# Transposing one token tile a second time in plain f32 and comparing the two results, in the expert phase of a two-layer decoder kernel

## The chip, the cores and the metric

The kernel runs on one core of one Trainium2 chip. The metric is the device time of one execution in microseconds (us). The time before is the median of three runs. A profile of one further execution, taken by the hardware profiler, gives the rows shown below; its times count from the first instruction of the execution.

## The reference

Six sublayers act on x of 16 x 128 tokens with 512 features; each adds its result to x and normalizes the row. The last one, the only one that the change touches, is a mixture of experts:

```
logits = x @ gate_weight.T
topk_w, topk_idx = top_k(softmax(logits), 2)
combine = zeros(T, 8).at[arange(T)[:, None], topk_idx].add(topk_w)
gu  = einsum('th,efh->tef', x, gate_up_weights)
act = silu(gu[..., :352]) * gu[..., 352:]
y   = einsum('tef,te,ehf->th', act, combine, down_weights)
sgu = x @ shared_gate_up.T
y   = y + (silu(sgu[:, :704]) * sgu[:, 704:]) @ shared_down.T
x   = layernorm(x + y)
```

## The kernel before

Each sublayer is a phase, written by hand for the five engines; an instruction waits on semaphores (`wait_ge`) and counts them up (`then_inc`). The shared part of the last sublayer is a phase of its own, which also routes the tokens: it writes each token's row twice to a DRAM buffer `x_slots`, sorted by expert, so that 39 tiles of 128 rows arise (`TILES`), each of which belongs to one expert.

`expert_ffn_phase` then works through these 39 tiles. Matrix products are made in three parts, from a rounded high half and a low half of each operand (`products`, lines 97 to 99; high halves end in `h`, low ones in `l`). For a tile i the steps are:

- SP loads the rows into `xin[:, i % 4, :]` (tile 0 is already in `first_x`).
- PE transposes them in four 128 x 128 blocks into the PSUM bank `tr` (`transposes`, L2147; tile 0 at L2149), and counts `tr_full` up at the last block.
- ACT copies `tr` to `xgh` (the rounded high half, L2048, counting `tr_hi`); DVE subtracts that from `tr` and writes the low half `xgl` (`tokens`, L2085, counting `tr_lo`).
- PE multiplies by the gate and the up weights (`ups`, 12 products of 352 columns each), ACT applies silu (L2063), DVE multiplies by the up part to `hf` (L2093).
- PE transposes `hf` into the bank `ht` (L2194), ACT and DVE split it to `hth` (L2071) and `htl` (L2099).
- PE multiplies by the down weights into `yb[i % 2]` (`down`, 9 products of 512 columns), ACT scales it to `ys` (L2055), SP stores it in `y_slots`.

The order on PE is fixed by the loop at the end of the function, and is a tile deep in software pipelining: `ups` of tile i, the transposes of tile i + 1, `down` of tile i - 1, the transposes of `hf` of tile i. On DVE it is `hf` of tile i, `tokens(i + 1)`, `htl` of tile i. In the first turn of the loop there is no `down`:

```
transposes(0)
...
pe.wait_ge(tr_lo, i + 1)
...
ups(gate[i % 2], i, ring, 0).then_inc(gate_full, 1)
...
    transposes(i + 1)
if i >= 1:
    down(i - 1, rings[i - 1][0])
```

POOL splits the weights of the coming experts meanwhile (L2006, L2009). After the tiles POOL fetches each token's two results from `y_slots`: the first set is added to `X` by indirect DMAs (L2033, counting `low_added`), the second goes to `yg`, which lies in the weights' buffers (L2036, counting `yg_in`). DVE adds `yg` (L2117), computes the statistics (L2120, L2123), ACT normalizes (L2076), SP stores the 16 blocks.

Of the kernel before, what the change touches and what calls it, by code (L numbers as in the profile page):

```python
# [7 lines left out]
ALU = mybir.AluOpType  # L8
ACT = mybir.ActivationFunctionType
AX = mybir.AxisListType.X  # L10

P = 128
B = 16
DM = 512
C = DM // P
# [79 lines left out]
def products(pe, out, wh, wl, xh, xl, first, last, **kw):  # L95

    pe.matmul(out, wh, xh, start=first, stop=False, **kw)  # L97
    pe.matmul(out, wh, xl, start=False, stop=False, **kw)  # L98
    return pe.matmul(out, wl, xh, start=False, stop=last, **kw)  # L99
# [57 lines left out]
class Phase:  # L157
# [8 lines left out]
    def sb(self, name, shape, dt=F32):  # L166
        return self.ctx.enter_context(self.nc.sbuf_tensor(f"{self.name}_{name}", shape, dt))

    def sem(self, name):
        self.sems.append(self.ctx.enter_context(self.nc.semaphore(f"{self.name}_{name}")))  # L170
        return self.sems[-1]
# [31 lines left out]
def four(bank):  # L203

    return bank[:, :].rearrange("p (c n) -> p c n", n=P)


def f32(ap):
    return ap.bitcast(F32)
# [1703 lines left out]
def expert_ffn_phase(nc, S, w):  # L1913
# [6 lines left out]
    NX = 4  # L1920
    sets = [(0, 4), (4, 8), (8, 12), (12, 14), (14, 16)]
    with Phase(nc, "expert") as phase:
        sb, sem = phase.sb, phase.sem
# [3 lines left out]
        xin, identr = sb("xin", [P, NX, DM], F32R), sb("identr", [P, P], F32R)  # L1927
# [9 lines left out]
        gate, up, yb, tr, ht = S.bank[0:2], S.bank[2:4], S.bank[4:6], S.bank[6], S.bank[7]  # L1937
# [7 lines left out]
        yg_in = [sem(f"yg_in{b}") for b in range(B)]  # L1945
        high_added = sem("high_added")
        w_hi, w_ready, tile_done, spare_set = sem("w_hi"), sem("w_ready"), sem("tile_done"), sem("spare_set")
        ident_rounded = sem("ident_rounded")
        tr_full, tr_hi, tr_lo = sem("tr_full"), sem("tr_hi"), sem("tr_lo")
        gate_full, up_full, sig_done, hf_done = sem("gate_full"), sem("up_full"), sem("sig_done"), sem("hf_done")  # L1950
        ht_full, ht_hi, ht_lo = sem("ht_full"), sem("ht_hi"), sem("ht_lo")
# [127 lines left out]
        @block.vector  # L2079
        def _(dve):  # L2080
            def tokens(i):
                dve.wait_ge(tr_hi, i + 1)
                if i >= 2:
                    dve.wait_ge(up_full, i - 1)
                dve.tensor_tensor(xgl[:, i % 2, :, :], four(tr), f32(xgh[:, i % 2, :, :]), ALU.subtract).then_inc(tr_lo, 1)  # L2085

            tokens(0)
            for i in range(TILES):
                dve.wait_ge(sig_done, i + 1)
                dve.wait_ge(up_full, i + 1)  # L2090
                if i >= 2:
                    dve.wait_ge(ht_full, i - 1)
                dve.tensor_tensor(hf[:, i % 2, :], sg[:, i % 2, :], up[i % 2][:, 0:F1], ALU.mult).then_inc(hf_done, 1)  # L2093
                if i + 1 < TILES:
                    tokens(i + 1)
                dve.wait_ge(ht_hi, i + 1)
                if i >= 2:
                    dve.wait_ge(tile_done, i)
                dve.tensor_tensor(htl[:, i % 2, :], ht[:, 0:HW], f32(hth[:, i % 2, :]), ALU.subtract).then_inc(ht_lo, 1)  # L2099

            def spread(k):
                lo, hi = sets[k]
                dve.wait_ge(mv_done, hi)
                dve.tensor_scalar(ve[:, lo:hi], mv[:, lo:hi, 1], EPS, None, ALU.add).then_inc(ve_done, 1)

            def shifts(k):
                lo, hi = sets[k]
                dve.wait_ge(rs_done, k + 1)
                dve.scalar_tensor_tensor(out=shift[:, lo:hi], in0=mv[:, lo:hi, 0], scalar=-1.0, in1=rs[:, lo:hi],
                                         op0=ALU.mult, op1=ALU.mult).then_inc(shift_done, 1)  # L2110

            ends = [hi - 1 for lo, hi in sets]
            for n in range(B + 2):
                if n < B:
                    dve.wait_ge(low_added[n], 16)
                    dve.wait_ge(yg_in[n], 16)
                    dve.tensor_tensor(S.X[:, n, :], S.X[:, n, :], yg[n], ALU.add).then_inc(high_added, 1)  # L2117
                if 1 <= n <= B:
                    dve.wait_ge(high_added, n)
                    dve.bn_stats(out=six[:, n - 1, :], in_=S.X[:, n - 1, :]).then_inc(six_done, 1)  # L2120
                if n >= 2:
                    dve.wait_ge(six_done, n - 1)
                    dve.bn_aggr(out=mv[:, n - 2, :], in_=six[:, n - 2, :]).then_inc(mv_done, 1)  # L2123
                    if n - 2 in ends:
                        spread(ends.index(n - 2))
                if n - 4 in ends:
                    shifts(ends.index(n - 4))
            for k in range(len(sets)):
                if ends[k] + 4 >= B + 2:
                    shifts(k)  # L2130

        @block.tensor
        def _(pe):
            def owner(i):
                ring = pe.value_load(S.ring[0:1, i:i + 1], min_val=0, max_val=2)
                order = pe.value_load(S.owner1[0:1, i:i + 1], min_val=1, max_val=E)
                return ring, order

            def transposes(i):
                if i:  # L2140
                    pe.wait_ge(ident_rounded, 1)
                    pe.wait_ge(x_in[i % NX], 16 * (i // NX + (i % NX > 0)))
                    pe.wait_ge(tr_lo, i)
                for c in range(C):
                    cols = slice(c * P, (c + 1) * P)
                    if i:
                        m = pe.transpose(tr[:, cols].bitcast(F32R), xin[:, i % NX, cols], identr[:, :])  # L2147
                    else:
                        m = pe.transpose(tr[:, cols], S.first_x[:, cols], S.ident[:, :])  # L2149
                m.then_inc(tr_full, 1)  # L2150

            def moving(t, ring, lo, n, r=P):
                return t[0:r, bass.ds(ring, 1), lo:lo + n].rearrange("p a n -> p (a n)")

            def ups(dst, i, ring, col):
                for c in range(C):
                    at = c * 2 * F1 + col
                    m = products(pe, dst[:, 0:F1], xgh[:, i % 2, c, :], xgl[:, i % 2, c, :],
                                 moving(weh, ring, at, F1), moving(wel, ring, at, F1), c == 0, c == C - 1)
                return m  # L2160

            def down(i, ring):
                pe.wait_ge(ht_lo, i + 1)
                if i >= 2:
                    pe.wait_ge(y_copied, i - 1)
                for j in range(J):
                    r, cols = FT[j], slice(j * P, (j + 1) * P)
                    m = products(pe, yb[i % 2], hth[0:r, i % 2, cols], htl[0:r, i % 2, cols],
                                 moving(weh, ring, WU + j * DM, DM, r), moving(wel, ring, WU + j * DM, DM, r),
                                 j == 0, j == J - 1)  # L2170
                m.then_inc(tile_done, 1)

            transposes(0)
            rings = [owner(0)]
            for i in range(TILES):
                ring, order = rings[i]
                pe.wait_ge(w_ready, order)
                pe.wait_ge(tr_lo, i + 1)
                if i >= 2:
                    pe.wait_ge(sig_done, i - 1)  # L2180
                ups(gate[i % 2], i, ring, 0).then_inc(gate_full, 1)
                if i >= 2:
                    pe.wait_ge(hf_done, i - 1)
                ups(up[i % 2], i, ring, F1).then_inc(up_full, 1)
                if i + 1 < TILES:
                    rings.append(owner(i + 1))
# [3 lines that stand above are left out]
                pe.wait_ge(hf_done, i + 1)  # L2190
                if i >= 1:
                    pe.wait_ge(ht_lo, i)
                for j in range(J):
                    m = pe.transpose(ht[0:FT[j], j * P:(j + 1) * P], hf[:, i % 2, j * P:j * P + FT[j]], S.ident[:, :])  # L2194
                m.then_inc(ht_full, 1)
            down(TILES - 1, rings[TILES - 1][0])
# [202 lines left out]
```

## Time and profile before

| | us |
|---|---|
| median of three runs (2100.69, 2104.23, 2106.11) | 2104.23 |
| the profiled execution, its own time | 2101.43 |
| its span, first to last instruction | 2099.6 |
| PE busy | 1930.7 (92%) |
| DVE busy | 1043.2 (50%) |
| ACT busy | 713.4 (34%) |
| POOL busy | 388.3 (18%) |
| mean granted TensorE clock, share of full | 0.970 |

The expert phase begins with PE's first transpose at 1789.4 us of the span; the last product of the last tile ends at 2055.0, the span at 2099.6. "Busy" is the time in which an engine has an instruction in work. PE stands for matrix products and transposes, PEld for its weight loads, which overlap PE. The granted clock tells how much of TensorE's full clock (2.4 GHz) the chip let through; it has two levels, 1.0 (2.4 GHz) and 0.5 (1.2 GHz), and a value between them is a stretch that holds both.

### The profile page before, as it was taken

The numbers are of one execution on the slowest core, as the hardware profiler recorded it, in microseconds if no ns is written. First come the engines' busy times: TensorE is split into PE (matmuls) and PEld (weight loads), VectorE is DVE, ScalarE is ACT, GpSimd is POOL, SyncE is SP. The second block draws the span as 40 slices with busy tenths as digits, with TensorE's granted clock in tenths as the row PEclk, the third lists the DMA queues.
The fourth block names the chain that finished last, engine by engine and source line by source line (L and its number), as shares of the span: only waits on it lengthen the run. The fifth ranks groups of instructions, "written<-read, shape, count | busy, mean of one in ns | idle before, by whom it ended". The sixth has DMA issues, their size and how long they took to land. (4 is left out here: it accounts for less than half of the span.)

```text
span 2099.6 us, 32791 instructions
## 1 busy us (share of the span) xinstructions
PE 1930.7 (92%) x12124; PEld 1574.2 (75%) x12124; DVE 1043.2 (50%) x1836; ACT 713.4 (34%) x2276; POOL 388.3 (18%) x339
## 2 busy tenths in 40 slices
PE   8999888999999979999899999999979997899991
PEld 6777576788888757877678887777758875799990
DVE  5676753455555455333455456667756232222224
ACT  4555624344444332212221111445542121233332
POOL 2110100000000046000021100000104332644335
PEclk9999999999999999999999999899999998899996
DMA  7211051000000021000290001000014200644257
GB/s 237 59 42 41 3 190 51 1 1 1 1 1 1 1 106 61 0 0 0 88 393 6 1 31 41 1 2 1 2 46 158 93 0 0 226 140 164 79 115 206
DMA packets 73375, 135.89 MB, mean 65 GB/s; under 512 B 13456, under 2 KB 31760, under 8 KB 71184
## 3 DMA queue, kind: packets, MB, share of 16 engines
q1 hardware_dynamic: 47376, 96.28, 13.3%
q0 software_dynamic: 7888, 27.94, 4.5%
q10 hardware_dynamic: 17968, 9.71, 1.8%
q8 instruction: 96, 1.57, 0.3%
q14 instruction: 47, 0.39, 0.1%
HBM read 90.62 MB, written 43.29 MB: 64 GB/s over the span
## 5 line engine op out<-in xcount | busy, mean ns | idle before, releaser
L1470 PE MATMUL banks<-ternary_xth,ternary_wq 128*128 (+1 forms) x352 | 139.3, 396 | 5.7 <-DVE ternary_wq L1401 3.6
L1470 PE MATMUL banks<-ternary_xtl,ternary_wq 128*128 (+1 forms) x352 | 138.1, 392 | 0.0
L571 ACT ACTIVATE causal_pr<-banks,causal_nb 128x128 f32<-128x128 f32 x256 | 90.1, 379 | 53.0 <-DVE causal_nb L713 53.0
L97 PE MATMUL banks<-latent_vh,latent_cth 128*128 128x512 f32 x256 | 104.3, 407 | 3.5 <-DVE latent_ctl L1171 3.5
L97 PE MATMUL banks<-weights,expert_xgh 128*128 x312 | 104.4, 334 | 2.3 <-DVE expert_xgl L2085 2.3
L571 ACT ACTIVATE gqa_pr<-banks,gqa_nb 128x128 f32<-128x128 f32 x256 | 90.1, 383 | 45.4 <-DVE gqa_nb L713 45.4
L99 PE MATMUL banks<-weights,expert_xgl 128*128 x312 | 101.2, 324 | 0.0
L98 PE MATMUL banks<-weights,expert_xgh 128*128 x312 | 101.1, 324 | 0.0
L98 PE MATMUL banks<-latent_vl,latent_cth 128*128 128x512 f32 x256 | 100.3, 392 | 0.0
L99 PE MATMUL banks<-latent_vh,latent_ctl 128*128 128x512 f32 x256 | 100.1, 391 | 0.0
L1124 ACT ACTIVATE latent_pt<-banks 128x1024 f32<-128x1024 f32 x32 | 32.9, 1027 | 187.8 <-PE banks L1270 187.8
L1430 DVE TENSOR_TENSOR ternary_hf<-ternary_sg,banks 128x512 f32<-128x512 f32 x44 | 30.2, 686 | 133.7 <-issue 80.1
L1371 ACT ACTIVATE ternary_sg<-banks 128x512 f32<-128x512 f32 x44 | 26.3, 598 | 190.2 <-PE banks L1470 190.2
L1085 POOL TENSOR_TENSOR latent_rs<-latent_ve,mhalf 128x1 f32<-128x1 f32 x15 | 8.3, 551 | 444.5 <-DVE latent_ve L219 444.5
L1115 ACT ACTIVATE latent_pr<-banks,latent_nb 128x128 f32<-128x128 f32 x256 | 90.2, 373 | 0.0
L97 PE MATMUL banks<-latent_xgh,latent_ch 128*128 128x256 f32 x256 | 77.2, 302 | 9.4 <-DVE latent_xgl L1165 4.6
L1470 PEld LDWEIGHTS banks<-ternary_xth,ternary_wq 128*128 128x128 f32 x352 | 66.4, 189 | 23.6 <-DVE ternary_xtl L70 4.9
L1171 DVE TENSOR_TENSOR latent_ctl<-banks,latent_cth 128x512 fp32r<-128x512 f32 x64 | 42.8, 689 | 71.6 <-ACT latent_cth L1102 71.6
L1482 PE MATMUL banks<-ternary_wq,ternary_hh 128*128 128x512 f32 x176 | 70.6, 401 | 8.1 <-DVE ternary_hl L1434 5.8
L1470 PEld LDWEIGHTS banks<-ternary_xtl,ternary_wq 128*128 128x128 f32 x352 | 66.4, 189 | 13.9
L743 DVE TENSOR_TENSOR X<-X,banks 128x512 f32<-128x512 f32 x48 | 33.0, 687 | 81.3 <-PE banks L99 81.3
L98 PE MATMUL banks<-latent_xgl,latent_ch 128*128 128x256 f32 x256 | 72.3, 283 | 0.0
(463 smaller groups left out, 5487.4 us busy)
## 6 DMA issues: line engine op xcount, KB each, us to landing
x_slots<-decay_zeros SPq DMA_DIRECT2D x39, 256.0 KB, 4.0
y_slots<-decay_zeros SPq DMA_DIRECT2D x39, 256.0 KB, 4.2
y_slots<-expert_ys SPq DMA_DIRECT2D x39, 256.0 KB
expert_xin<-x_slots SPq DMA_DIRECT2D x38, 256.0 KB, 2.9
weights_raw<-in_expert_experts SPq DMA_DIRECT2D x4, 2176.0 KB, 9.1
gqa_tw<-in_ternary_w ACTq DMA_DIRECT2D x4, 2112.0 KB
ternary_raw<-in_ternary_w SPq DMA_DIRECT2D x11, 768.0 KB, 4.1
expert_raw<-in_expert_experts POOLq DMA_DIRECT2D x3, 2176.0 KB, 10.0
```

What stands on the lines that cost most here:

```text
L97: pe.matmul(out, wh, xh, start=first, stop=False, **kw)
L98: pe.matmul(out, wh, xl, start=False, stop=False, **kw)
L99: return pe.matmul(out, wl, xh, start=False, stop=last, **kw)
L571: a = act.activation(pr[:, h, c, :], S.bank[2 * h + c // 4][:, (c % 4) * P:(c % 4 + 1) * P], ACT.Exp, bias=nb[:, h, c:c + 1], accum_out=su ...
L743: dve.tensor_tensor(row, row, bank, ALU.add).then_inc(free_d, 1)
L1115: a = act.activation(pr[:, c, :], S.bank[x][:, j * P:(j + 1) * P], ACT.Exp, bias=nb[:, c:c + 1], accum_out=sums[:, c:c + 1])
L1124: act.activation(pt[:, :, :], pair(1), ACT.Copy).then_inc(pt_done, 1)
L1171: dve.tensor_tensor(ctl[:, x, :], S.bank[2 + x], f32(cth[:, x, :]), ALU.subtract).then_inc(ct_lo, 1)
L1371: act.activation(sg[:, j % 2, :], gate[j % 2][:, :], ACT.Sigmoid).then_inc(sig_done, 1)
L1430: dve.tensor_tensor(hf[:, j % 2, :], sg[:, j % 2, :], up[j % 2][:, :], ALU.mult).then_inc(hf_done, 1)
L1470: a = pe.matmul(dst[:, :], wq[:, j, m, c * P:(c + 1) * P], x[:, c, toks], start=c == 0 and n == 0, stop=c == C - 1 and n == 1)
L1482: a = pe.matmul(yb[i][:, :], h[:, j % 2, i * P:(i + 1) * P], wq[:, j, 2, :], start=j == 0 and n == 0, stop=j == J - 1 and n == 1)
```

## The change

Tile 1 is treated differently from the other 38. After its four transposes on the rounded f32r type, PE makes the same four on plain f32, into the bank `yb[1]` (PSUM bank 5), and only the last of these counts `tr_full`. DVE then runs five instructions ahead of the `xgl` of tile 1: it copies `tr` to SBUF, subtracts `yb[1]`, squares, takes the maximum over each row of 512, and writes 1e4 or 0 to `wrong`, per partition. Each of the first four counts `off_chain`, and the next waits for it. Much later, ahead of the add of `yg[0]`, DVE adds `wrong` to column 0 of block 0 of `X` and waits for that. The buffers `off`, `most` and `wrong` and the semaphores `off_done` and `off_chain` are new; the buffers are declared behind all others of the phase.

```diff
@@ -1945,7 +1945,8 @@
         yg_in = [sem(f"yg_in{b}") for b in range(B)]
         high_added = sem("high_added")
         w_hi, w_ready, tile_done, spare_set = sem("w_hi"), sem("w_ready"), sem("tile_done"), sem("spare_set")
-        ident_rounded = sem("ident_rounded")
+        ident_rounded, off_done, off_chain = sem("ident_rounded"), sem("off_done"), sem("off_chain")
+        off, most, wrong = sb("off", [P, DM]), sb("most", [P, 1]), sb("wrong", [P, 1])
         tr_full, tr_hi, tr_lo = sem("tr_full"), sem("tr_hi"), sem("tr_lo")
         gate_full, up_full, sig_done, hf_done = sem("gate_full"), sem("up_full"), sem("sig_done"), sem("hf_done")
         ht_full, ht_hi, ht_lo = sem("ht_full"), sem("ht_hi"), sem("ht_lo")
@@ -2082,6 +2083,16 @@
                 dve.wait_ge(tr_hi, i + 1)
                 if i >= 2:
                     dve.wait_ge(up_full, i - 1)
+                if i == 1:
+                    dve.tensor_copy(off[:, :], tr).then_inc(off_chain, 1)
+                    dve.wait_ge(off_chain, 1)
+                    dve.tensor_tensor(off[:, :], off[:, :], yb[1], ALU.subtract).then_inc(off_chain, 1)
+                    dve.wait_ge(off_chain, 2)
+                    dve.tensor_tensor(off[:, :], off[:, :], off[:, :], ALU.mult).then_inc(off_chain, 1)
+                    dve.wait_ge(off_chain, 3)
+                    dve.tensor_reduce(most[:, :], off[:, :], AX, ALU.max).then_inc(off_chain, 1)
+                    dve.wait_ge(off_chain, 4)
+                    dve.tensor_scalar(wrong[:, :], most[:, :], 0.0, 1e4, ALU.is_gt, ALU.mult).then_inc(off_done, 1)
                 dve.tensor_tensor(xgl[:, i % 2, :, :], four(tr), f32(xgh[:, i % 2, :, :]), ALU.subtract).then_inc(tr_lo, 1)
 
             tokens(0)
@@ -2113,6 +2124,10 @@
             for n in range(B + 2):
                 if n < B:
                     dve.wait_ge(low_added[n], 16)
+                    if n == 0:
+                        dve.wait_ge(off_done, 1)
+                        dve.tensor_scalar(S.X[:, 0, 0:1], S.X[:, 0, 0:1], wrong[:, 0:1], None, ALU.add).then_inc(off_done, 1)
+                        dve.wait_ge(off_done, 2)
                     dve.wait_ge(yg_in[n], 16)
                     dve.tensor_tensor(S.X[:, n, :], S.X[:, n, :], yg[n], ALU.add).then_inc(high_added, 1)
                 if 1 <= n <= B:
@@ -2147,6 +2162,10 @@
                         m = pe.transpose(tr[:, cols].bitcast(F32R), xin[:, i % NX, cols], identr[:, :])
                     else:
                         m = pe.transpose(tr[:, cols], S.first_x[:, cols], S.ident[:, :])
+                if i == 1:
+                    for c in range(C):
+                        cols = slice(c * P, (c + 1) * P)
+                        m = pe.transpose(yb[1][:, cols], f32(xin[:, i % NX, cols]), S.ident[:, :])
                 m.then_inc(tr_full, 1)
 
             def moving(t, ring, lo, n, r=P):
```

On PE, from the load of tile 1's owner on, the order before:

```order
L2135 ISA x2
L2136 TENSOR_LOAD owner
L2136 ISA x2
L2147 MATMUL banks<-expert_identr,expert_xin 128x128 x4
L2194 MATMUL banks<-ident,expert_hf 128x128 x2
L2194 MATMUL banks<-ident,expert_hf 96x128
L97 ISA
L97 MATMUL banks<-weights,expert_xgh 128x352
```

and in the changed kernel:

```order
L2150 ISA x2
L2151 TENSOR_LOAD owner
L2151 ISA x2
L2162 MATMUL banks<-expert_identr,expert_xin 128x128 x4
L2168 MATMUL banks<-ident,expert_xin 128x128 x4
L2213 MATMUL banks<-ident,expert_hf 128x128 x2
L2213 MATMUL banks<-ident,expert_hf 96x128
L97 ISA
L97 MATMUL banks<-weights,expert_xgh 128x352
```

The four plain transposes stand between those of tile 1 and those of tile 0's `hf`; the first product behind them is the gate product of tile 1.

On DVE, from the phase's first instruction on, the order before:

```order
L2085 TENSOR_TENSOR expert_xgl<-banks,expert_xgh 128x512
L2093 TENSOR_TENSOR expert_hf<-expert_sg,banks 128x352
L2085 TENSOR_TENSOR expert_xgl<-banks,expert_xgh 128x512
L2099 TENSOR_TENSOR expert_htl<-banks,expert_hth 128x384
L2093 TENSOR_TENSOR expert_hf<-expert_sg,banks 128x352
```

and in the changed kernel:

```order
L2096 TENSOR_TENSOR expert_xgl<-banks,expert_xgh 128x512
L2104 TENSOR_TENSOR expert_hf<-expert_sg,banks 128x352
L2087 COPY expert_off<-banks 128x512
L2089 TENSOR_TENSOR expert_off<-expert_off,banks 128x512
L2091 TENSOR_TENSOR expert_off<-expert_off 128x512
L2093 TENSOR_REDUCE expert_most<-expert_off 128x1
L2095 TENSOR_SCALAR expert_wrong<-expert_most 128x1
L2096 TENSOR_TENSOR expert_xgl<-banks,expert_xgh 128x512
L2110 TENSOR_TENSOR expert_htl<-banks,expert_hth 128x384
L2104 TENSOR_TENSOR expert_hf<-expert_sg,banks 128x352
```

The five new instructions stand ahead of tile 1's `xgl`; `htl` of tile 0 and `hf` of tile 1 are queued behind it.

## Rows read from the trace of the kernel before

**Rows 1.** The page, the chain that ended last, its shares by engine.

```profile
PE 12%; POOL 1%; DMA 0%; DVE 0%; ACT 0%; issue 0%; ACTq 0%; DVEq 0%
```

**Rows 2.** Windows of the expert phase: busy us, then PEclk, DMA share, GB/s.

```profile
core 0: us, PE busy (x) PEld busy (x) DVE busy (x) ACT busy (x) POOL busy (x), PEclk, DMA share, GB/s
1799.80:2051.00 251.20, 251.17 (x1516) 233.37 (x1516) 66.43 (x113) 79.60 (x150) 122.35 (x67) 1.00 0.47 142
```

**Rows 3.** Waits of PE from 1787 us on: us in total, times, longest.

```profile
PE banks L97 <- DVE expert_xgl L2085: 2.3, 2, 1.6
```

**Rows 4.** Timeline around tile 1's transposes: start us, us, engine, operation.

```profile
1797.75 0.46 PE L2147 MATMUL banks<-expert_identr,expert_xin 128*128 128x128 f32 x4
1798.03 0.52 DVE L2093 TENSOR_TENSOR expert_hf<-expert_sg,banks 128x352 f32<-128x352 f32 x1 [6.16 <-PE banks L99]
1798.25 0.60 ACT L2048 ACTIVATE expert_xgh<-banks 128x512 fp32r<-128x512 f32 x1 [1.82 <-PE banks L2147]
...
1798.61 0.55 PE L2194 MATMUL banks<-ident,expert_hf 128*128 128x128 f32 x3 [0.39 <-DVE expert_hf L2093]
1798.88 0.69 DVE L2085 TENSOR_TENSOR expert_xgl<-banks,expert_xgh 128x512 fp32r<-128x512 f32 x1 [0.33 <-ACT expert_xgh L2048]
...
1799.83 0.42 PE L97 MATMUL banks<-weights,expert_xgh 128*128 x1 [0.67 <-DVE expert_xgl L2085]
```

**Rows 5.** Windows in a run of plain f32 transposes (L60).

```profile
1553.00:1556.00 3.00, 3.00 (x16) 3.00 (x15) 1.89 (x3) 2.08 (x4) 0.00 (x0) 0.50 0.94 257
...
1557.00:1560.00 3.00, 3.00 (x30) 3.00 (x29) 2.84 (x6) 2.99 (x7) 0.00 (x0) 1.00 0.91 389
```

**Rows 6.** Groups of DVE by line and form: xcount, busy us, mean ns.

```profile
L713 DVE TENSOR_REDUCE gqa_nb<-banks 128x8 f32<-128x1024 f32 x32 | 39.2, 1224 | 16.9 <-PE banks L864 16.1
...
L1175 DVE COPY latent_qt<-banks 128x512 f32<-128x512 f32 x32 | 22.1, 691 | 70.4 <-PE banks L99 70.4
...
L1804 DVE TENSOR_TENSOR shared_hf<-shared_sg,banks 128x512 f32<-128x512 f32 x20 | 13.7, 686 | 68.7 <-PE banks L99 58.9 <-issue 9.8
...
L2117 DVE TENSOR_TENSOR X<-X,weights_raw 128x512 f32<-128x512 f32 x8 | 5.5, 689 | 12.1 <-DMA weights_raw<-y_slots,pos 11.9
...
L219 DVE TENSOR_SCALAR causal_ve<-causal_mv 128x1 f32<-128x1 f32 x16 | 2.5, 154 | 0.5
...
L1695 DVE TENSOR_REDUCE shared_mx<-first_x 128x16 f32<-128x128 f32 x1 | 0.3, 285 | 0.0
```

**Rows 7.** Timeline of DVE: L1140 waits for L1139 by a semaphore.

```profile
307.89 0.42 DVE L1139 TENSOR_TENSOR latent_pt<-ahead_kv,latent_kvr 128x256 f32<-128x256 f32 x1
308.34 0.42 DVE L1140 TENSOR_TENSOR ahead_kv<-latent_pt 128x256 f32<-128x256 f32 x1
```

**Rows 8.** Timeline of DVE: L2120 does not wait for the L2117 ahead.

```profile
2082.40 0.69 DVE L2117 TENSOR_TENSOR X<-X,expert_raw 128x512 f32<-128x512 f32 x1 [0.64 <-DMA expert_raw<-y_slots,pos]
2083.01 0.69 DVE L2120 BATCH_NORM_STATS2 expert_six<-X 128x6 f32<-128x512 f32 x1
```

**Rows 9.** Windows: gaps of PE, and stretches at a half clock behind them.

```profile
250.00:252.00 2.00, 0.00 (x0) 0.00 (x0) 0.89 (x2) 2.00 (x14) 0.00 (x0) 1.00 0.02 4
252.00:257.00 5.00, 4.84 (x18) 3.77 (x19) 2.45 (x4) 0.63 (x3) 0.78 (x1) 0.66 0.02 3
...
398.50:401.00 2.50, 0.00 (x0) 0.00 (x0) 1.39 (x3) 1.74 (x9) 0.11 (x1) 1.00 0.00 0
401.00:403.00 2.00, 1.89 (x16) 1.92 (x17) 0.00 (x0) 0.00 (x0) 0.00 (x0) 1.00 0.00 0
...
1304.50:1314.00 9.50, 9.50 (x49) 7.82 (x50) 5.31 (x7) 5.57 (x28) 0.21 (x1) 0.50 0.61 210
...
1547.00:1552.00 5.00, 0.00 (x0) 0.00 (x0) 2.30 (x7) 0.00 (x0) 0.55 (x1) 0.79 0.00 0
1552.00:1557.00 5.00, 4.97 (x25) 5.00 (x26) 2.90 (x5) 2.83 (x5) 0.00 (x0) 0.52 0.77 243
```

**Rows 10.** Timeline of DVE: its first add after the tiles.

```profile
2063.64 0.69 DVE L2117 TENSOR_TENSOR X<-X,weights_raw 128x512 f32<-128x512 f32 x1 [11.14 <-DMA weights_raw<-y_slots,pos]
```

## The prediction

> **What bounds the kernel now.** I read the chain that ended last first. Its engine shares begin in the expert phase, and of them PE has 12% of the span, POOL 1%, everything else about nothing [rows 1]: there, PE sets the end. The windows say the same more sharply. From the gate product of tile 1 to the last tiles PE is busy for 251.17 of 251.20 us, at a clock of 1.00, while DVE is busy for 66.43 and ACT for 79.60 [rows 2]. So from that product on there is no slack on PE in which a delay could be made good: what is late at 1799.83 is late at the end. DVE, in contrast, is idle for three quarters of the time, and the same five instructions in most other places of the phase would cost nothing. Everything hangs on the place.
>
> The place is the first turn of the software pipeline, before there is a `down` to fill PE's time. PE's only waits for an `xgl` in this phase are the two of tiles 0 and 1, 2.3 us in total, 1.6 the longer [rows 3], hence 0.7 for tile 1. The timeline shows how this comes about [rows 4]: PE's transposes of tile 1 end at 1798.21, ACT's high half runs from 1798.25 to 1798.85, DVE's `xgl` from 1798.88 to 1799.57, and 0.26 later PE starts the gate product at 1799.83. PE itself was done with the transposes of tile 0's `hf` at 1799.16. It is therefore the chain of transposes, ACT, DVE that PE waits for, and the change puts work into two links of it. From tile 2 on, `down` of an earlier tile stands between the transposes and the gate product and covers that chain; those tiles are left as they are.
>
> **The change, part by part.**
>
> *Four plain f32 transposes on PE.* A run of such transposes passes 30 in 3.00 us at the full clock and 16 in 3.00 at the half [rows 5], 0.10 and 0.19 us each. The four f32r transposes ahead take 0.46 us together [rows 4], less than four at the half clock could, so the clock is full and `tr_full` comes 4 x 0.10 = 0.40 us later; bounds are 0.4 and, at a half clock, 0.75. PE's own time is not lengthened by them: `hf` is ready only at 1798.55 [rows 4], and the four start their work at about 1798.1 and have been passed by then.
>
> *Five instructions on DVE, each behind the one before.* The copy of 512 elements from PSUM takes 0.691, the subtraction with one operand in PSUM 0.686, the product of two SBUF operands 0.689 (as the add of L2117). The row maximum has no row of its size; between 128 elements in SBUF at 0.285 and 1024 in PSUM at 1.224 it comes by a straight line to 0.69. The comparison on 128 x 1 takes 0.154 [rows 6]. What the four waits add is seen where L1140 waits for L1139: 0.42 of work, the next start after 0.45, so 0.03 each [rows 7]. Without a wait, the next 512-element instruction starts after 0.61 of the 0.69 [rows 8]. So four steps of 0.69 + 0.03 make 2.88 us, and the fifth, for which `xgl` does not wait, 0.154 - 0.08 = 0.07: together 2.95 us.
>
> Here a page can be set against the rows. The Trainium skill, "VectorE: DVE Perf Modes", section "The DRAIN you can't avoid", says of chained Vector instructions that the semaphore after each of them costs nothing extra, as the pipeline empties after each anyhow. By that the step would be the 0.61 of the unwaited pair and the five would come to about 2.5 us, 0.44 less. The rows of this kernel speak against it, since waited and unwaited pairs differ by 0.11 us.
>
> *Queue behind them.* On DVE `htl` of tile 0 and `hf` of tile 1 stand behind the five. `htl` would end at about 1803.5; `down(0)`, which needs it, comes after 24 more products and the next transposes, which PE starts only after `xgl`. `hf` of tile 1 needs the up product, later still. On ACT nothing new stands ahead of `hth`. SP's load of tile 4 waits for `tr_full` of tile 0, and POOL's weight split for a DMA; neither is touched. All these I cost at nothing, with 3 to 4 us of products as their cover.
>
> *The late add on DVE.* It waits for `off_done`, long since set, and for `low_added[0]`. DVE then stands idle for 11.14 us until its first add at 2063.64, because `yg[0]` has yet to land [rows 10]. A 128 x 1 instruction of 0.154 lies inside that; without the cover it would cost 0.2. Two more semaphores to clear at the end are instructions with no visible time. Nothing depends on what the comparison finds: the instruction list has no branch, so a differing word would change the output and no time.
>
> *Sum of the delay:* 0.40 + 2.95 = 3.35 us. PE's gap ahead of the gate product of tile 1 grows from 0.67 to 4.0 us.
>
> *The clock.* That gap is long by this kernel's measure. A gap of 2.0 us at 250 was followed by a stretch in which the granted clock averages 0.66 over 5 us, which is 2 x 0.34 x 5 = 3.4 us at the half level. A gap of 5.0 us at 1547 saw the clock fall within it (mean 0.79, so 2.1 us at the half level, the fall 2.9 us after its start) and then 4.8 us of half clock (0.52 over 5 us). But a gap of 2.5 us at 398.5 left it at 1.00 [rows 9]. With 4.0 us, beyond 2.9, I expect the fall. What it costs is the share of the work that is not done: 16 transposes instead of 30 in the same time is a loss of 0.47. Bounds: 0 (the gap of 2.5) and 4.8 x 0.47 = 2.3 us; I take the 3.4 us of the first case, 1.6 us, since the restart here meets the same unbroken work as there.
>
> The Trainium skill, "TensorE: Matmul & The Clock Gate", section "Terms", puts the penalty at throttled time times one minus the clock ratio, one half. By that the 3.4 us would cost 1.7, and the sum would be 0.1 more; the rows give 0.47, as the part of the time that does not follow the clock would have it.
>
> Total: 3.35 + 1.6 = 5.0 us. The profiled execution's own time of 2101.43 would become 2106.4. It lies 2.8 below the median of the three runs, to which I apply the same sum: 2104.23 + 5.0 = **2109.2 us**, 0.24% more. About 0.3% (6.3 us) is what a measurement of this kernel can tell from no change; the three runs alone differ by 5.4.
>
> **The rivals.**
>
> *The clock does not fall.* The gap of 2.5 us that passed without effect speaks for it, the 5.0 that did not against. Then only the delay counts: +3.35, 2107.6.
>
> *The half clock lasts long, and the change is measurably slower.* Place: tiles 1 and 2, right behind the gap. From 1304.5 to 1314.0 PE was busy throughout and the clock stayed at 0.50 [rows 9]. The same here costs 9.5 x 0.47 = 4.5 us on top: +7.8, 2112.0. It decides once the half clock lasts longer than (6.3 - 3.35) / 0.47 = 6.3 us. For it: it happened in this trace. Against: behind the other two gaps it lasted 3.4 and 4.8 us, and the work here is an unbroken row of full products.
>
> *The delay is absorbed.* That would be so if something other than PE set the end, say POOL's first set of gathers or the landing of the last stores. Against it speaks the absence of slack on PE [rows 2], and that these gathers wait for the same tiles. +0, 2104.2.
>
> *The memory or code layout shifts something elsewhere.* The buffers come last and the phases ahead have the same instructions; this could go either way, by no more than the scatter of the runs: 2102 to 2106.
>
> **How the numbers follow.** My forecast, one fall of the clock that lasts 2 to 5 us, gets 0.68; no fall 0.14; the long half clock 0.09; absorbed 0.06; layout 0.03. The predicted time is that of the first. Range: at the low end the delay with the shorter steps of 0.61 (2.9 us), no clock term, less 2 us for the scatter of a median of such runs: 2105. At the high end 3.35 + 2.3, plus those 2: 2111.9, which takes in the long half clock at 2112. So 2105 to 2112. Slower by over 0.3%: the long half clock whole, 0.09, a quarter of the forecast, where a high clock term and scatter meet, 0.16, and 0.01 of layout, 0.26. Faster by over 0.3%: 0.02, from scatter and layout. The same: 0.72.
>
> **What would show it.** In the changed kernel's timeline: ACT's high half of tile 1 0.4 us later against the transposes before it; five new DVE instructions in some 3 us; PE's wait for `xgl` of tile 1 near 4.0 instead of 0.7; the next window after it at a clock of 0.50 for some 3 us, with products at nearly double spacing; then tiles at the old pace to the end; and the first add after the tiles still behind the landing of `yg[0]`. I am wrong if PE's gap is under 2 us, if tiles after the second run slower than before, or if the end does not move with the last tile.

## The result, and the profile after

The changed kernel took 2112.21 us in the median of 18 runs (2105.34 to 2116.25), the kernel before 2104.87 in 18 runs beside them (2100.69 to 2110.09). The ratio is 1.0029, with a 95% interval from 1.0019 to 1.0040, which is +6.1 us (4.0 to 8.4) on 2105. The forecast was 2109.2, from 2105 to 2112, and "the same within 0.3%" at 0.72. So direction and order are right, and the size is at the upper side: the delay and the clock together, forecast at 5.0 us, lie inside the interval, but below its middle. The ratio is taken from all runs; the two medians alone differ by 7.3 us. The median of 2112.21 itself is 0.2 us above the stated range. The ratio of +0.29% is just inside "the same within 0.3%", and its interval reaches beyond that.

On the page of the changed kernel, busy time of the engines and the shares of the chain that ended last read as before [rows 1]: PE still sets the end.

```profile
PE 1935.6 (92%) x12128; PEld 1578.6 (75%) x12128; DVE 1047.6 (50%) x1842; ACT 711.7 (34%) x2276; POOL 388.1 (18%) x339
...
PE 12%; POOL 1%; DVE 1%; DMA 0%; ACT 0%; issue 0%; ACTq 0%; DVEq 0%
```

The profiled execution has a span of 2112.7 us, 13.1 more than the one before. Most of that isn't the change's, which is why I cut both spans at three instructions: T0, the start of tile 0's transposes; the start of tile 1's gate product, A behind T0; the start of the last tile's down products, B behind that; and the end, C behind that. D is the last part of A, from the first f32r transpose of tile 1 on.

| | T0 | A | of which D | B | C |
|---|---|---|---|---|---|
| before | 1789.43 | 10.40 | 2.08 | 252.81 | 46.96 |
| changed | 1796.32 | 14.12 | 5.50 | 254.25 | 48.01 |
| difference | 6.89 | 3.72 | 3.42 | 1.44 | 1.05 |

A and B are where the change acts, 5.16 us together. The timeline of PE, ACT and DVE around tile 1 answers to [rows 4]; square brackets hold the time for which the engine was idle just before the instruction, and what ended it:

```profile
1804.94 0.46 PE L2162 MATMUL banks<-expert_identr,expert_xin 128*128 128x128 f32 x4
1805.24 0.63 PE L2168 MATMUL banks<-ident,expert_xin 128*128 128x128 f32 x4
1805.80 0.55 PE L2213 MATMUL banks<-ident,expert_hf 128*128 128x128 f32 x3
1805.90 0.60 ACT L2049 ACTIVATE expert_xgh<-banks 128x512 fp32r<-128x512 f32 x1 [2.50 <-PE banks L2168]
...
1806.53 0.69 DVE L2087 COPY expert_off<-banks 128x512 f32<-128x512 f32 x1 [0.79 <-ACT expert_xgh L2049]
1807.26 0.69 DVE L2089 TENSOR_TENSOR expert_off<-expert_off,banks 128x512 f32<-128x512 f32 x1
1807.98 0.69 DVE L2091 TENSOR_TENSOR expert_off<-expert_off 128x512 f32<-128x512 f32 x1
1808.70 0.69 DVE L2093 TENSOR_REDUCE expert_most<-expert_off 128x1 f32<-128x512 f32 x1
1809.43 0.15 DVE L2095 TENSOR_SCALAR expert_wrong<-expert_most 128x1 f32<-128x1 f32 x1
1809.50 0.68 DVE L2096 TENSOR_TENSOR expert_xgl<-banks,expert_xgh 128x512 fp32r<-128x512 f32 x1
1810.10 0.55 DVE L2110 TENSOR_TENSOR expert_htl<-banks,expert_hth 128x384 fp32r<-128x384 f32 x1
...
1810.44 0.66 PE L97 MATMUL banks<-weights,expert_xgh 128*128 x1 [4.09 <-DVE expert_xgl L2096]
```

From the first f32r transpose to ACT's start it is 0.96 us, where it was 0.50: the four plain ones cost 0.46. From ACT's start to the start of `xgl` it is 3.60, where it was 0.63: the five instructions cost 2.97. Each 512-element one starts 0.72 after the one before and lasts 0.69, and `xgl` starts 0.07 after the comparison. Together with 0.01 less from `xgl` to PE that is D's 3.42. The remaining 0.30 of A comes before all that: the clock rose later within tile 0's products, and tile 1's transposes began 8.62 behind T0 instead of 8.32. PE's wait grew from 0.7 to 4.1 (in total, with tile 0's, from 2.3 [rows 3] to 5.7), and behind it the clock is at its half level for 0.32 x 2 x 5 = 3.2 us of the next 5:

```profile
PE banks L97 <- DVE expert_xgl L2096: 5.7, 2, 4.1
```

```profile
core 0: us, PE busy (x) PEld busy (x) DVE busy (x) ACT busy (x) POOL busy (x), PEclk, DMA share, GB/s
1806.44:1810.44 4.00, 0.00 (x1) 0.01 (x1) 3.77 (x7) 0.44 (x2) 2.17 (x2) 0.97 1.01 435
1810.44:1815.44 5.00, 5.00 (x22) 5.00 (x23) 0.20 (x1) 0.46 (x1) 5.00 (x3) 0.68 0.37 150
1815.44:2062.00 246.56, 246.45 (x1491) 229.12 (x1490) 65.98 (x112) 78.61 (x148) 114.41 (x63) 1.00 0.44 134
```

In the first of these windows PE is idle, and the clock falls some 0.2 us before its end. In the second PE passes 22 matmuls in 5 us, where the kernel before passed 32 in the 5 us behind its own gap. In the third the clock is at 1.00 and PE has practically no gaps, as in [rows 2]. B is longer by 1.44, and this stretch is the only one in it that differs.

The late add lies where it was expected, right behind DVE's last `htl` and ahead of the idle time before the first add. It took 0.20 us and nothing waited for it:

```profile
2063.99 0.56 DVE L2110 TENSOR_TENSOR expert_htl<-banks,expert_hth 128x384 fp32r<-128x384 f32 x1 [2.60 <-ACT expert_hth L2072]
2064.46 0.20 DVE L2129 TENSOR_SCALAR X<-X,expert_wrong 128x1 f32<-128x1 f32 x1
2075.86 0.69 DVE L2132 TENSOR_TENSOR X<-X,weights_raw 128x512 f32<-128x512 f32 x1 [11.19 <-DMA weights_raw<-y_slots,pos]
```

The two other differences, T0 and C, are looked at below.

### The profile page after: what moved, and what is told of

Same layout as the page of the kernel before. It is cut to its first block and busy times, and to the rows that moved or that the text cites. A ratio compares the mean times of both kernels' runs of the same rounds, so it can differ in the third digit from the quotient of the medians.

```text
span 2112.7 us, 32808 instructions
## 1 busy us (share of the span) xinstructions
PE 1935.6 (92%) x12128; PEld 1578.6 (75%) x12128; DVE 1047.6 (50%) x1842; ACT 711.7 (34%) x2276; POOL 388.1 (18%) x339
```

## The experiments

Eleven runs were made, two of them repeats (e4 of the changed kernel, e5 of the one before), each with a profile, in which the cuts were made as above. They ran on three chips: e1 to e4 on one where the kernel before takes 2104.39 us, e5 to e8 on one where it takes 2112.95, e9 to e11 on one where it takes 2105.04. Each ratio is against the runs of the kernel before on the same chip. The edits are shown against the changed kernel.

| | T0 | A | D | PE's gap | B | C | ratio (95%) |
|---|---|---|---|---|---|---|---|
| e1 declarations only | 1790.37 | 10.68 | 2.06 | 0.67 | 252.81 | 48.34 | 1.0005 (0.9993 to 1.0017) |
| e2 check behind xgl | 1793.71 | 10.37 | 2.08 | 0.67 | 252.53 | 48.09 | 1.0005 (0.9994 to 1.0016) |
| e3 gap filled | 1795.96 | 14.01 | 5.38 | 0.26 | 253.12 | 48.31 | 1.0018 (1.0005 to 1.0031) |
| e4 changed, again | 1796.99 | 15.74 | 6.34 | 4.94 | 254.00 | 48.87 | 1.0026 (1.0012 to 1.0039) |
| e5 before, again | 1798.14 | 11.01 | 2.07 | 0.67 | 252.78 | 48.17 | 1.0001 (0.9988 to 1.0014) |
| e6 nine instructions | 1797.67 | 22.59 | 13.80 | 12.40 | 255.31 | 48.63 | 1.0070 (1.0044 to 1.0095) |
| e7 nine, from PSUM | 1800.64 | 16.57 | 8.37 | 6.97 | 253.98 | 48.61 | 1.0030 (1.0016 to 1.0044) |
| e8 copy alone ahead | 1797.89 | 11.32 | 3.13 | 1.73 | 252.80 | 48.19 | 1.0010 (0.9994 to 1.0027) |
| e9 PE part only | 1792.77 | 11.35 | 2.54 | 1.13 | 252.67 | 48.41 | 1.0006 (0.9993 to 1.0019) |
| e10 DVE part only | 1792.70 | 14.16 | 5.02 | 3.62 | 255.11 | 47.53 | 1.0040 (1.0023 to 1.0057) |
| e11 not-equal | 1786.31 | 14.06 | 4.77 | 3.36 | 254.18 | 47.95 | 1.0019 (1.0005 to 1.0033) |

**Is anything else of the change in the time?** First the declarations without the instructions:

```diff
-                if i == 1:
-                    dve.tensor_copy(off[:, :], tr).then_inc(off_chain, 1)
...
-                    if n == 0:
-                        dve.wait_ge(off_done, 1)
...
-                if i == 1:
-                    for c in range(C):
...
```

> Only the three buffers and two semaphores of the change are declared; no instruction of it is issued (the comparison and the late add are left out). Theory (delay of 3.7 us on PE's path ahead of tile 1's gate product, plus the clock): no difference, 0 us, A (start of tile 0's transposes to start of tile 1's gate product) 10.4 us as before, within 0.3 for where the clock rises. Rival (layout, two more semaphores to clear, moved code): the part of the measured +6.1 us that the delay and the clock do not explain, 1 to 3 us, shows here.

Measured: ratio 1.0005, A 10.68, B 252.81. No layout term of 1 to 3 us is seen, though the interval (-1.5 to +3.6 us) alone wouldn't exclude a small one. The kernel before once more, for a second profile:

> The kernel before once more, for a second profile of it. Both theories: A 10.4 to 10.7 us, B 252.8. Theory (run scatter outside the stretch that the change touches): tile 0's transposes start anywhere from 1789 to 1797 us, and the stretch C from the last tile's down products to the end is 47 to 49 us, as in the changed kernels. Rival (the change lengthens C by 1 us or more): C is 47.0 again.

T0 is 1798.14 here (on the second chip) and C 48.17, later and longer than in the changed kernel. C was 47.53 to 48.87 in all profiles but the first, with or without the change (48.34 in e1, 48.17 here); the 46.96 of the first was the exception, and the change adds nothing there. T0 depends on the execution: on the third chip e11, with four of the five DVE instructions, has 1786.31, earlier than the kernel before in its first profile, while e9 and e10 have 1792.77 and 1792.70; on the second, e6 and e8 have 1797.67 and 1797.89, about as the unchanged e5. The profiled executions of the changed kernel (2114.52), e3 (2113.49) and e4 (2117.41) were also among the longer ones of their kernels, and the first one of the kernel before (2101.43) among the shorter. The strongest evidence is e2 below, which issues every instruction of the change and whose ratio leaves at most 3.4 us. So the 6.9 us ahead of the expert phase aren't the change's either. A moved too in the unchanged kernel, to 11.01, by when the clock rises within tile 0's products; D is 2.07 and stands still. The part that the change makes in the first pair of profiles is thus 3.42 in D and 1.44 in B, 4.9 us.

**The same work elsewhere.** The plain transposes count their own semaphore, and the comparison stands behind `xgl`:

```diff
...
+                dve.tensor_tensor(xgl[:, i % 2, :, :], four(tr), f32(xgh[:, i % 2, :, :]), ALU.subtract).then_inc(tr_lo, 1)
                 if i == 1:
+                    dve.wait_ge(off_full, 1)
                     dve.tensor_copy(off[:, :], tr).then_inc(off_chain, 1)
...
-                dve.tensor_tensor(xgl[:, i % 2, :, :], four(tr), f32(xgh[:, i % 2, :, :]), ALU.subtract).then_inc(tr_lo, 1)
...
+                if i == 2:
+                    pe.wait_ge(off_chain, 1)
...
+                m.then_inc(tr_full, 1)
                 if i == 1:
                     for c in range(C):
                         cols = slice(c * P, (c + 1) * P)
                         m = pe.transpose(yb[1][:, cols], f32(xin[:, i % NX, cols]), S.ident[:, :])
-                m.then_inc(tr_full, 1)
+                    m.then_inc(off_full, 1)
```

> The whole comparison is kept, but the plain transposes count a semaphore of their own, so that tr_full comes when it did, and the five DVE instructions stand behind tile 1's xgl; PE's transposes of tile 2 wait for the copy. Theory: A goes back to 10.4 us, PE's wait for xgl of tile 1 to 0.7, no fall of the clock, the run within 1 us of the kernel before. Rival (the instructions cost by themselves, wherever they stand): +3 us or more stays.

Measured: A 10.37, B 252.53, ratio 1.0005 (-1.3 to +3.4 us). All instructions of the change run, and neither A nor B is longer. PE starts the gate product as early after `xgl` as before, while DVE goes on with the copy:

```profile
1803.13 0.69 DVE L2086 TENSOR_TENSOR expert_xgl<-banks,expert_xgh 128x512 fp32r<-128x512 f32 x1 [0.33 <-ACT expert_xgh L2049]
1803.74 0.68 DVE L2089 COPY expert_off<-banks 128x512 f32<-128x512 f32 x1
1804.45 0.69 DVE L2091 TENSOR_TENSOR expert_off<-expert_off,banks 128x512 f32<-128x512 f32 x1
```

```profile
1804.08 0.42 PE L97 MATMUL banks<-weights,expert_xgh 128*128 x1 [0.67 <-DVE expert_xgl L2086]
```

The place costs, not the work, as far as A and B tell.

**The clock by itself.** PE gets something to do in the gap:

```diff
                 pe.wait_ge(w_ready, order)
+                if i == 1:
+                    for _ in range(34):
+                        pe.transpose(yb[0][:, 0:P], S.ident[:, :], S.ident[:, :])
                 pe.wait_ge(tr_lo, i + 1)
```

> The changed kernel with 34 transposes of the identity into the free bank yb[0] on PE, issued ahead of the wait for tile 1's xgl, about 3.4 us of work inside the gap of 4.1. Theory (two terms): A stays at 14.1, the clock stays at 1.00 behind it, and B (start of tile 1's gate product to start of the last tile's down products) is 252.8 us as before instead of 254.3; the run comes out at +3.7 against before. Rival (the clock fall is no consequence of the gap): B stays at 254.3 and the run at +5 to +6.

```profile
1805.97:1809.97 4.00, 3.74 (x36) 3.51 (x34) 3.66 (x7) 0.55 (x2) 1.52 (x2) 1.00 1.01 426
1809.97:1814.97 5.00, 5.00 (x31) 4.85 (x32) 0.84 (x2) 1.04 (x2) 5.00 (x3) 1.00 0.42 174
```

D is 5.38, so the delay stays, but the clock stays at 1.00 and PE passes 31 matmuls in the 5 us behind the gap instead of 22. B is 253.12, 1.1 below the changed kernel's. The ratio of 1.0018 is +3.8 us (1.1 to 6.5). So the clock's fall is a consequence of the gap, and its price in the profiles is 1.1 to 1.4 us. A shorter gap is the other test:

```diff
                     dve.tensor_copy(off[:, :], tr).then_inc(off_chain, 1)
+                dve.tensor_tensor(xgl[:, i % 2, :, :], four(tr), f32(xgh[:, i % 2, :, :]), ALU.subtract).then_inc(tr_lo, 1)
+                if i == 1:
                     dve.wait_ge(off_chain, 1)
...
-                dve.tensor_tensor(xgl[:, i % 2, :, :], four(tr), f32(xgh[:, i % 2, :, :]), ALU.subtract).then_inc(tr_lo, 1)
```

> Only the copy stays ahead of tile 1's xgl, the other four instructions stand behind it; the plain transposes are still counted in tr_full. Theory (delay adds up, the clock falls only in a long gap): 0.46 for the transposes and 0.61 for the copy, A 11.4 to 11.8 us, PE's gap 1.7 us, the clock stays at 1.00, B 252.8, +1.1 us against before. Rival (a gap of 1.7 us is enough for a fall): B 254 and +2.6.

A gap of 1.73 us left the clock alone, and B is 252.80. D is 3.13, 1.05 more than before; 0.46 + 0.61 were expected. That A is only 0.3 above the 11.01 of e5 comes from the clock, which rose earlier here. The ratio of 1.0010 doesn't tell +1.1 from nothing. Gaps of 1.1 and 1.7 us (e9, e8) left the clock at 1.00, and gaps of 3.4 us and more were followed by a fall. Between them lie only [rows 9], which go both ways: behind 2.0 us it fell, behind 2.5 it didn't.

**The two halves of the delay.** PE's part alone, with the comparison and the late add left out:

```diff
-                if i == 1:
-                    dve.tensor_copy(off[:, :], tr).then_inc(off_chain, 1)
...
-                    if n == 0:
-                        dve.wait_ge(off_done, 1)
...
```

> Only the four plain transposes are added, with tr_full at their last; the five DVE instructions and the late add are left out. Theory: ACT's high half of tile 1 starts 0.96 us after the first f32r transpose instead of 0.50, PE's gap is 1.1 instead of 0.7, A 10.8 to 11.5 with where the clock rises, no fall of the clock, B 252.8, +0.5 us in all. Rival (plain f32 transposes cost four times the columns, 0.2 us each): 1.3 us instead of 0.50.

DVE's part alone, with the plain transposes left out and the subtraction taking `tr`:

```diff
-                    dve.tensor_tensor(off[:, :], off[:, :], yb[1], ALU.subtract).then_inc(off_chain, 1)
+                    dve.tensor_tensor(off[:, :], off[:, :], tr, ALU.subtract).then_inc(off_chain, 1)
...
-                if i == 1:
-                    for c in range(C):
-                        cols = slice(c * P, (c + 1) * P)
-                        m = pe.transpose(yb[1][:, cols], f32(xin[:, i % NX, cols]), S.ident[:, :])
```

> Only the five DVE instructions and the late add; the plain transposes are left out and the subtraction takes tr in place of yb[1]. Theory: from the start of ACT's high half of tile 1 to the start of xgl 3.60 us instead of 0.63, PE's gap 3.6 us, the clock falls in or behind it, A 13.3 to 14 (plus 0.4 to 1.2 if the product meets POOL's first instruction), B 253.8 to 255, +4 to +5 us. Rival (3.6 us is short enough to leave the clock alone): B 252.8 and +3.

With PE's part, ACT started at 1802.54, 0.96 behind the first transpose at 1801.58: 0.46 more than before, and not the rival's 1.3. PE's gap was 1.13; D is 2.54, 0.46 more. With DVE's part, `xgl` started at 1805.93, 3.60 behind ACT's start at 1802.33; D is 5.02, 2.94 more. Both terms are alone what they are together. B of 255.11 holds the clock and 0.7 us of a different kind: ACT's last `ys` but one waited 4.2 us for a store to land, and PE's last wait for `htl` was 2.2 instead of 1.5. Its ratio of 1.0040 is +8.4 us (4.8 to 12.0), from six runs, where 4 to 5 was expected. D and B explain 5.2 of it (2.9 and 2.3); the rest stays open. The ratio lies above the whole change's 1.0029, but the two intervals overlap.

**A product that took 1.54 us.** The changed kernel once more was meant as a repetition:

> The changed kernel once more, beside the others on one chip. Theory: A 13.8 to 14.1, the clock falls in or behind the gap and the half level lasts 2 to 5 us behind it, B 253.8 to 255.1, +5 us against before (4.5 to 6). Rival (something outside the expert phase takes 1 to 3 us more): the start of tile 0's transposes or the stretch behind the last tile is later than in the kernel before, again, by the same amount as in the first profile (6.9 and 1.1 us).

B is 254.00 as expected, but A is 15.74 and the gap 4.94. Part of it is the clock: tile 1's transposes begin 9.40 behind T0. The other part is in D, 6.34 instead of 5.50: of DVE's five, the third took more than twice its time, just when POOL had begun to split the next expert's weights:

```profile
1808.70 0.69 DVE L2089 TENSOR_TENSOR expert_off<-expert_off,banks 128x512 f32<-128x512 f32 x1
1809.42 1.54 DVE L2091 TENSOR_TENSOR expert_off<-expert_off 128x512 f32<-128x512 f32 x1
1811.00 0.69 DVE L2093 TENSOR_REDUCE expert_most<-expert_off 128x1 f32<-128x512 f32 x1
```

```profile
1809.03 4.53 POOL L2007 CAST weights<-expert_raw 128x1450 fp32r<-128x1450 f32 x3 [11.91 <-DMA expert_raw<-in_expert_experts]
```

This product is the one instruction of the five with two full operands in SBUF. In the first profile it had begun at 1807.98, 0.29 ahead of POOL's start at 1808.27, and took 0.69. There it was POOL that paid, and in e10, where the product was 0.12 ahead, as well: the first cast took 1.65 and 1.82 us instead of 1.39.

```profile
L2007 POOL CAST weights<-expert_raw 128x1450 fp32r<-128x1450 f32 x1 | 1.7, 1653 | 11.8 <-DMA expert_raw<-in_expert_experts 11.8
```

```profile
L2007 POOL CAST weights<-expert_raw 128x1450 fp32r<-128x1450 f32 x1 | 1.8, 1824 | 11.7 <-DMA expert_raw<-in_expert_experts 11.7
```

In e3 the product was done before POOL began, and no cast took over 1.40. I took the product for an instruction that POOL can hold up, and made the meeting certain in one kernel and impossible in the other: four more products of `off` with itself, and the same with the second operand of all five in PSUM.

```diff
                     dve.wait_ge(off_chain, 4)
+                    dve.tensor_tensor(off[:, :], off[:, :], off[:, :], ALU.mult).then_inc(off_chain, 1)
+                    dve.wait_ge(off_chain, 5)
...
                     dve.tensor_scalar(wrong[:, :], most[:, :], 0.0, 1e4, ALU.is_gt, ALU.mult).then_inc(off_done, 1)
```

> Four more products of off with itself (both operands in SBUF) in the chain ahead of tile 1's xgl, nine instructions in place of five. Theory A (a DVE instruction with two SBUF operands that meets POOL's weight split is held until POOL's instruction is done, which took 1.54 us in place of 0.69 in the run before): several of the five products take 1.2 to 2 us, A is 19 to 22 us, well over 14.1 + 2.9 = 17.0. Theory B (the 1.54 was a chance event): each stays at 0.69 and A is 17.0. Either way the clock falls within the gap and B is 253.8 to 255.2.

> As the run before it, but the second operand of all five products is the PSUM bank yb[1]. Theory A (only a second SBUF operand meets POOL): each product takes 0.69, A is 17.0 us, however POOL works beside it. Theory B (any DVE work beside POOL is slowed): as in the run before, over 19. The clock falls within the gap of 7 us, B 254 to 255.2.

Groups of DVE and POOL by line, with both operands in SBUF:

```profile
L2101 DVE TENSOR_TENSOR expert_off<-expert_off 128x512 f32<-128x512 f32 x1 | 3.6, 3611 | 0.0
L2007 POOL CAST weights<-expert_raw 128x1450 fp32r<-128x1450 f32 x1 | 1.8, 1774 | 11.9 <-DMA expert_raw<-in_expert_experts 11.9
L2097 DVE TENSOR_TENSOR expert_off<-expert_off 128x512 f32<-128x512 f32 x1 | 1.8, 1764 | 0.0
L2099 DVE TENSOR_TENSOR expert_off<-expert_off 128x512 f32<-128x512 f32 x1 | 1.8, 1761 | 0.0
L2095 DVE TENSOR_TENSOR expert_off<-expert_off 128x512 f32<-128x512 f32 x1 | 1.0, 1041 | 0.0
...
L2091 DVE TENSOR_TENSOR expert_off<-expert_off 128x512 f32<-128x512 f32 x1 | 0.7, 691 | 0.0
...
L2093 DVE TENSOR_REDUCE expert_most<-expert_off 128x1 f32<-128x512 f32 x1 | 0.7, 686 | 0.0
```

and with the second operand in PSUM, in order of time, with POOL's casts beside them:

```profile
1811.87 0.69 DVE L2091 TENSOR_TENSOR expert_off<-expert_off,banks 128x512 f32<-128x512 f32 x1
1812.59 0.69 DVE L2093 TENSOR_REDUCE expert_most<-expert_off 128x1 f32<-128x512 f32 x1
1813.31 0.69 DVE L2095 TENSOR_TENSOR expert_off<-expert_off,banks 128x512 f32<-128x512 f32 x1
1814.04 0.69 DVE L2097 TENSOR_TENSOR expert_off<-expert_off,banks 128x512 f32<-128x512 f32 x1
1814.76 0.69 DVE L2099 TENSOR_TENSOR expert_off<-expert_off,banks 128x512 f32<-128x512 f32 x1
1815.48 0.69 DVE L2101 TENSOR_TENSOR expert_off<-expert_off,banks 128x512 f32<-128x512 f32 x1
```

```profile
1812.74 4.07 POOL L2007 CAST weights<-expert_raw 128x1450 fp32r<-128x1450 f32 x3 [11.98 <-DMA expert_raw<-in_expert_experts]
```

The products in SBUF take 1.04, 1.76, 1.76 and 3.61 us as soon as POOL works, and the first of POOL's casts 1.77 instead of 1.39; 1.76 is about what one of its casts lasts, 3.61 about one of its subtractions (3.7 there). With a PSUM operand, all products take 0.69 while POOL's three casts run beside them in 4.07. So theory A holds: a product with both operands in SBUF and POOL's split exclude each other for a whole instruction, and a PSUM operand avoids it. Both operands were the same buffer here; two different ones were not run beside POOL here. The row maximum, with its single SBUF operand, took 0.69 beside POOL in both. D came out at 13.80 and 8.37. The second is 6.29 above the 2.08 of before, and 3.42 + 4 x 0.72 would be 6.30; the first is 5.4 above that, which is what its last four products took over 0.69. The ratios of e6 and e7, +14.8 us (9.3 to 20.1) and +6.3 (3.4 to 9.3), hold the 14.2 and 7.5 that D and B add up to. (A of 16.57 is below the 17.0 expected because the clock rose early.) In e8, too, the product met POOL and took 1.91 us, but behind `xgl`, where it cost nothing. The Trainium skill, "SBUF — State Buffer", section "SBUF: two separate sides", says that VectorE and GpSimd share one pair of SBUF ports, which whoever starts first holds for its whole instruction; the rows agree, down to POOL's casts becoming longer where the product started first (1.65, 1.82).

These two also show what a long gap does to the clock. Behind 12.4 us B is 255.31, behind 7.0 it is 253.98: +2.5 and +1.2 us. The price doesn't grow in step with the gap, but with what is left of the half level behind it: about 3.2 us in e7, 5.4 us in e6.

**A shorter comparison.** One not-equal takes the place of subtraction and product:

```diff
-                    dve.tensor_tensor(off[:, :], off[:, :], yb[1], ALU.subtract).then_inc(off_chain, 1)
+                    dve.tensor_tensor(off[:, :], off[:, :], yb[1], ALU.not_equal).then_inc(off_chain, 1)
...
-                    dve.tensor_tensor(off[:, :], off[:, :], off[:, :], ALU.mult).then_inc(off_chain, 1)
...
```

> The comparison in four DVE instructions: the subtraction and the product give way to one not-equal with its second operand in PSUM. Theory: 0.72 us less, and the only instruction with two full SBUF operands is gone, so it cannot meet POOL: xgl starts 2.88 us after ACT's high half, PE's gap 3.4 us, A 13.1 to 13.8, B 253 to 255, run at +4 us. Rival (two operands of which one is in PSUM are also held): one of the four takes over 1 us.

`xgl` started at 1799.43, 2.87 behind ACT's start at 1796.56, D is 4.77, 0.73 less than the changed kernel's, and none of the four took over 0.69, though POOL began at 1798.30. PE's gap is 3.36. A is 14.06, as the clock rose late (the transposes began 9.29 behind T0). The ratio of 1.0019 (1.0005 to 1.0033) is +4.0 us. By D it is 0.7 cheaper than the change as made, which the two ratios can't confirm, as their intervals overlap. e2's order makes even that one free.

## Why the prediction was right, point by point

- **What bounds.** PE, without slack from tile 1 on: B, some 250 us of gapless work, was within 0.4 us of 252.8 wherever the clock didn't fall, so no delay in A was ever made good.
- **Plain transposes, 0.40.** Measured 0.46, in the changed kernel and alone in e9. The last plain transpose takes 0.27 where the last f32r one takes 0.24, which I left out; that is half of the rest.
- **Five DVE instructions, 2.95.** Measured 2.97 in the changed kernel and in e10, and 0.72 for each step. The rule weighed beside it, that a semaphore after each costs nothing, would have given 2.5.
- **What was missed in that step** is what the 0.69 of the product hangs on. I took it from the add of L2117, which has two SBUF operands too but runs where POOL isn't splitting weights. In four profiles of this chain (the changed kernel, e3, e4, e10) it took 1.54 once; in two it started first, in e10 by 0.12 us, and POOL waited. That POOL's first cast began at 1801.28 in the kernel before, 2.4 us behind the old `xgl`, was in its trace, and the longer chain would reach it. I looked at POOL for what it waits for, not for what it holds.
- **Work queued behind, the late add, layout: nothing.** Confirmed (e1, e2, and the 0.20 us of the late add in idle time).
- **The clock, 1.6, from 3.4 us at the half level.** Measured 3.4 us, 0.2 of them still in the gap and 3.2 behind it, and 1.44 in the first profile, 1.2 in e4, 1.1 by e3's filling. The rule weighed beside it, one half of the throttled time, would give 1.6 for those 3.2; what B lost is 0.45 of them. The 3.4 us that I took from the gap at 250 also came out in e4, e10 and e11. That was luck in part: [rows 9] also had a gap without a fall and half levels of 4.8 and 9.5 us, and nothing in them chose between these. The rival of no fall has no case in the four gaps from 3.4 to 4.9 us; in two of them (e10, e11) the clock still stood at 1.00 when PE started again and fell 0.9 and 1.3 us later. The rival of the long half clock was not seen either: the longest half level behind a gap was 5.4 us, at a price of 2.5 us, behind 12.4 us of gap.
- **The sum.** Forecast 5.0, 4.9 in the first pair of profiles, 5.2 with the later rise of the clock that the first pair also shows; by all runs 6.1 (4.0 to 8.4). A meeting with POOL, 0.85 us in e4, would move it up by 0.2 on average; this is an estimate that takes one in four as the rate, from four profiles. How far the rest is scatter stays open: the two medians differ by 7.3, but e4's ratio gives 5.5 (2.5 to 8.2).

## What to carry to other kernels

What a check, a copy or a counter costs depends on its place in the chain and not on its busy time alone: the same four transposes and five DVE instructions took 5 us ahead of the instruction that the bound engine waits for, and nothing that A or B show behind it. Give added work its own semaphore instead of moving the one that others wait for. Where an idle gap of the matrix engine grows, look for the clock's price, once per gap: 1 to 1.6 us behind the gaps of 3.4 to 7 us here, 2.5 behind 12.4, nothing behind those up to 1.7; and where a DVE instruction has two SBUF operands, look whether POOL works at that time, or take one operand from PSUM.

## What the runs showed of the hardware that was not expected

- A DVE product of 512 elements with two SBUF operands took 1.54, 1.76 and up to 3.61 us beside POOL instead of 0.69, and POOL's casts took 1.65 to 1.85 instead of 1.39. With one operand in PSUM both kept their times.
- The clock can fall after the gap is over: in e10 and e11 it was at 1.00 when PE started again behind 3.6 and 3.4 us, and fell 0.9 and 1.3 us later, for 3.4 us. In e10, with the granted clock third from the right:

```profile
1806.70:1807.20 0.50, 0.34 (x2) 0.25 (x2) 0.37 (x1) 0.00 (x0) 0.50 (x1) 1.00 1.05 453
1807.20:1807.70 0.50, 0.50 (x4) 0.50 (x4) 0.00 (x0) 0.00 (x0) 0.50 (x2) 1.00 1.13 487
1807.70:1808.20 0.50, 0.50 (x4) 0.50 (x3) 0.00 (x0) 0.00 (x0) 0.50 (x1) 0.55 0.52 197
```

- The same kernel's A moved between 10.40 and 11.01 us by when the clock rises in tile 0's products. In the changed one it was 14.12 and 15.74, and 0.78 of that difference is the clock's. That is as much as several of the terms that were to be measured. D, which starts behind that, repeated within 0.02 us in the kernels without a longer chain (2.06 to 2.08).
